# Batch 0's dispatch softmax with tokens in the partitions, in a two-layer attention and slot-expert kernel

## The chip, the cores and the metric

One core of a Trainium2 chip runs the whole program. The metric is the device time of one execution, in microseconds.

## What is computed

The input is `x` of 2 batches by 2048 tokens by 256 features, fp32. First layer: `x = x + layernorm(attention(layernorm(x)))`, an attention of 16 heads with 32 learned patterns in which a sparsemax takes the place of the softmax. Second layer: `x = x + layernorm(slots(layernorm(x)))`, in which 16 slots per batch look at all tokens, go each through an expert of its own, and all tokens look at the 16 slots:

```python
q = jnp.broadcast_to(slot_query, (Bx, NS, D))
o = q + _mha(q, x, x, d_Wq, ...)              # dispatch: 16 slots over 2048 tokens, 16 heads
h = _layernorm(o.reshape(Bx, E, S, D), ...)   # one slot an expert
y = einsum('besf,efd->besd', silu(h @ e_W1 + e_b1) * silu(h @ e_Wg + e_bg), e_W2) + e_b2
o = o + y
out = _mha(x, o, o, c_Wq, ...)                # combine: 2048 tokens over 16 slots
```

The change concerns the dispatch of batch 0. 16 heads times 16 slots make 256 rows ("columns" after the change) of scores over 2048 tokens, each with a softmax over the tokens.

## The kernel before

The four thousand tokens are cut into 32 tiles of 128, in 8 groups of 4 (groups 0 to 3 are batch 0, 4 to 7 batch 1). Every engine has its own program, written out by hand in the order in which it runs; engines wait for each other by counted semaphores (`wait_ge`, `then_inc`). There is no scheduler: what stands in a row on an engine runs in that row, and a wait holds all that stands behind it.

Until about 180 us the kernel makes the sparsemax scores. Then TensorE goes through the heads of batch 1 in steps n = 16 to 33 (the loop `for n in range(KT, 2 * KT + 2)` in the TensorE program, at L1390). Step n has `turn_a(n)` (4 transposes, L1147), `mix(n-1)` (L1157) and `project(n-2)` (L1168), each with a copy by ScalarE between them: `take_a` (L837), `take_h` (L843). VectorE takes the result in `keep_output(n-2)` (L1885, L1887, and L1891 once in four), ScalarE normalises a finished group in `norm_o(g)`, VectorE adds it to `x` and takes its statistics in `join(g)` (L1901, L1656, L1659), GpSimd makes the roots (`roots`, L629 to L634) and ScalarE makes the second norm, `second_norm(g)` (L776), the input of the second layer.

Between these steps lies the dispatch. For a group g, TensorE turns the normed tokens (`turn_norm`, L1194), ScalarE copies them (`put_norm`, L869), TensorE makes the scores (`slot_scores`, L1202: slots in the partitions, 512 tokens in a row, two halves m of 128 slots), and ScalarE keeps them in `s_all` (`put_slot_scores`, L875). VectorE takes each half's maximum over the row (`group_maximum`, L1914). With all four groups of batch 0 there, `batch_maximum` makes one maximum a row (L1918, L1920) and ScalarE makes the exponentials of all 2048 tokens with their sum (`exponential`, L879, twice). The probabilities have slots in the partitions, but the product with the tokens sums over tokens, so they are turned: `turn_p(n)` (four transposes, L1217), copied by `put_probabilities(n)` (L897), and used by `mix_p(n)` (L1231), n = 0 to 7 for batch 0, 8 to 15 for batch 1. `to_slots(0, step)` makes the slots of it. Batch 1 goes the same way in two parts, groups 4 and 5 early (`early_maximum`, `exponential_of_part(False, m)`, L885), 6 and 7 late.

SyncE starts all loads of expert weights (`fetch(n)`) into places that come free, in a fixed row, each behind the wait that frees its place. 21 places are filled ahead of the experts, which start at about 302 us; the later loads wait for `up_ps` or `down_ps` of earlier experts. At the end, from about 400 us, the combine runs.

In the rows, `keep_output(30)` is the L1885 at 239.76 us, `project(n)` is a pair of L1168, and PEld is the weight load that belongs to a PE row.

## Time and profile before

| | us |
|---|---|
| median of 3 runs | 463.04 |
| lowest, highest | 462.29, 465.19 |
| the profiled execution, its own time | 461.39 |
| its span in the profile | 459.7 |
| TensorE busy | 397.7 (87%) |
| VectorE busy | 310.2 (67%) |
| ScalarE busy | 225.3 (49%) |
| GpSimd busy | 147.3 (32%) |

The profile is of one execution, which was 1.65 us faster than the median. The span leaves out 1.7 us at the ends. Busy shares are means over stages with different limits, so they do not say what bounds a stage.

### The profile page before, as it was taken

The page shows a single profiled execution, that of the slowest core. Times are in us where ns is not written, and L with a number is a line of the kernel's source. Part 1 is how long each engine was busy: PE and PEld are TensorE (multiplying, and loading weights), DVE is VectorE, ACT ScalarE, POOL GpSimd, SP SyncE. Part 2 cuts the span into 40 slices and gives each one's busy share as a digit, 9 for nine tenths or more (in the row PEclk, how much of TensorE's full clock was granted, in tenths as well). Part 3 has the DMA queues.
Part 4 walks back from the last instruction along what each step waited for, and adds up shares of the span by engine and source line. Part 5 has one row for each costly group of instructions (what it writes and reads, how often), then busy time and mean ns, then how long its engine had stood idle before and what let it go on. Part 6 is the DMA issues. An engine that isn't in the chain of part 4 may idle for free. (4 is left out here: it accounts for less than half of the span.)

```text
span 459.7 us, 6977 instructions
## 1 busy us (share of the span) xinstructions
PE 397.7 (87%) x2086; PEld 245.7 (53%) x2086; DVE 310.2 (67%) x1189; ACT 225.3 (49%) x413; POOL 147.3 (32%) x243
## 2 busy tenths in 40 slices
PE   7987757589799988999999898999998679999983
PEld 4543223235455454665867666634443237888872
DVE  4899899989999986675425324333334125979996
ACT  2445746748778787878575633100000010355761
POOL 4134465482957522333212100010000000345353
PEclk9997787979989998999999899999999899999999
DMA  7931011011010228448539936979999999701215
GB/s 246 289 124 46 1 46 46 1 46 48 1 46 3 75 97 280 147 151 285 185 135 324 364 139 218 365 249 400 385 404 377 397 378 344 282 0 47 85 54 183
DMA packets 45055, 83.78 MB, mean 182 GB/s; under 512 B 2007, under 2 KB 36445, under 8 KB 40797
## 3 DMA queue, kind: packets, MB, share of 16 engines
q1 hardware_dynamic: 44722, 83.16, 51.7%
q8 instruction: 17, 0.28, 0.2%
q10 hardware_dynamic: 298, 0.21, 0.2%
q14 instruction: 18, 0.14, 0.1%
HBM read 70.78 MB, written 12.58 MB: 181 GB/s over the span
## 5 line engine op out<-in xcount | busy, mean ns | idle before, releaser
L1135 PE MATMUL bank<-Wz,yT 128*128 128x512 f32 x128 | 70.3, 701 | 19.1 <-DVE top L1739 18.9
L1135 PEld LDWEIGHTS bank<-Wz,yT 128*128 128x128 f32 x128 | 27.9, 226 | 54.7 <-issue 44.9
L1739 DVE MAX8 top<-bank 128x8 f32<-128x32 f32 x512 | 51.6, 178 | 1.3 <-ACT arena L798 1.1
L1071 ACT ACTIVATE d<-d 128x32 f32<-128x32 f32 x16 | 3.7, 229 | 84.7 <-DVE d L2127 84.7
L1168 PE MATMUL bank<-aWo,hoT 128*128 128x256 f32 x128 | 37.0, 412 | 0.2 <-DVE arena L1885 0.2
L738 POOL TENSOR_TENSOR work<-work 128x512 f32<-128x512 f32 x16 | 16.6, 1059 | 63.1 <-DVE work L2202 63.1
L1231 PE MATMUL bank<-d,work 128*128 128x256 f32 x128 | 31.9, 397 | 1.6 <-ACT d L897 1.6
L629 POOL TENSOR_SCALAR veps<-mv 128x4 f32<-128x4 f32 x24 | 5.9, 244 | 78.6 <-DVE mv L1659 53.7
L1591 PE MATMUL bank<-scr,work 128*128 128x256 f32 x128 | 29.1, 381 | 1.6 <-ACT work L1084 1.6
L1202 PE MATMUL bank<-arena,Wd 128*128 128x512 f32 x64 | 29.2, 599 | 1.5 <-ACT arena L869 1.5
L1567 PE MATMUL bank<-scr,arena 128*128 128x256 f32 x128 | 28.9, 380 | 0.0
L776 ACT ACTIVATE arena<-arena,shift,rstd 128x256 f32<-128x256 f32 x52 | 26.9, 595 | 3.5 <-POOL shift L634 3.5
L1231 PEld LDWEIGHTS bank<-d,work 128*128 128x128 f32 x128 | 25.2, 205 | 4.9 <-ACT d L897 2.1
L1168 PEld LDWEIGHTS bank<-aWo,hoT 128*128 128x128 f32 x128 | 22.2, 193 | 9.8 <-issue 6.2
L1591 PEld LDWEIGHTS bank<-scr,work 128*128 128x128 f32 x128 | 24.2, 190 | 5.3 <-ACT work L1084 2.1
L2116 DVE TENSOR_TENSOR d<-bank,slotT 128x4 f32 (+1 forms) x16 | 2.6, 165 | 35.2 <-PE bank L1497 35.2
L1157 PE MATMUL bank<-heads 128*64 128x256 f32 x128 | 21.8, 420 | 4.6 <-ACT heads L837 2.6
L632 POOL TENSOR_TENSOR rstd<-veps,mhalf 128x4 f32<-128x4 f32 x24 | 24.9, 1037 | 2.0
L1567 PEld LDWEIGHTS bank<-scr,arena 128*128 128x128 f32 x128 | 23.6, 190 | 3.5 <-DVE scr L2160 0.3
L1885 DVE TENSOR_TENSOR arena<-bank,Wz 128x256 f32<-128x256 f32 x16 | 6.7, 421 | 25.3 <-PE bank L1168 25.2
L1479 PE MATMUL bank<-arena,top 128*32 128x512 f32 x96 | 21.0, 598 | 2.2 <-DMA above<-in_L_ffn_e_Wg_dram 2.2
L659 POOL TENSOR_TENSOR d<-arena,past 128x1024 f32<-128x1024 f32 x8 | 15.1, 1912 | 24.0 <-DVE past L1753 24.0
(295 smaller groups left out, 880.6 us busy)
## 6 DMA issues: line engine op xcount, KB each, us to landing
arena<-in_L_ffn_e_W_dram SPq DMA_DIRECT2D x10, 1024.0 KB, 8.4
x<-in_L_ffn_e_W_dram SPq DMA_DIRECT2D x7, 1024.0 KB, 6.3
scr<-in_L_ffn_e_W_dram SPq DMA_DIRECT2D x7, 1024.0 KB, 13.7
arena<-in_L_ffn_e_Wg_dram SPq DMA_DIRECT2D x6, 1024.0 KB, 9.7
work<-in_L_ffn_e_W_dram SPq DMA_DIRECT2D x5, 1024.0 KB, 12.5
x<-in_L_attn_query_dram SPq DMA_DIRECT2D x1, 4096.0 KB, 16.5
out_dram<-x SPq DMA_DIRECT2D x8, 512.0 KB, 4.4
...
```

Source lines behind the costliest of these rows:

```text
L632: pool.tensor_tensor(rstd[:, k, :], veps[:, k, :], mhalf[:, :], ALU.pow).then_inc(root[k], 1)
L738: pool.tensor_tensor(pv, pv, crs[:, u * 32:(u + 1) * 32].unsqueeze(2).broadcast_to([P, 32, NE]), ALU.mult)\
L776: return act.activation(dst, src, ACT.Identity, bias=shift[:, k, t:t + 1], scale=rstd[:, k, t:t + 1])
L1135: mm = pe.matmul(bZ[t % 2][:, :], yT[:, c, t * P:(t + 1) * P], Wz[:, c, :], start=(c == 0), stop=(c == C - 1))
L1157: mm = pe.matmul(psH[64 * a:64 * a + 64, :], bdh[:, n % TG, :], quarter[:, :, a, :], start=True, stop=True)
L1168: mm = pe.matmul(psO, hoT[:, n % 2, m, :], aWo[:, m, :], start=(m == 0 and n >= KT), stop=(m == 1))
L1202: mm = pe.matmul(bT[m][:, :], Wd[:, c, m * P:(m + 1) * P], ynT[:, g, c, :], start=(c == 0), stop=(c == C - 1))
L1231: mm = pe.matmul((bZ[0] if n < 8 else bank[7])[:, c * 2 * P:(c + 1) * 2 * P], yn[:, kt, c::C], pT[:, n % 2, u * 2 * P:(u + 1) * 2 * P], st ...
L1479: mm = pe.matmul(bank[q][32 * k:32 * k + 32, :], hcol[:, q, c, :], pair[g][c][half], start=(c == 0), stop=(c == C - 1))
L1567: mm = pe.matmul(ps, ynT[:, j, c, t * P:(t + 1) * P], Wc[:, b, c, :], start=(c == 0), stop=(c == C - 1))
L1591: mm = pe.matmul(ps, cpT[:, u, (v * 2 + m) * P:(v * 2 + m + 1) * P], Vc[:, b, m, :], start=(m == 0), stop=(m == 1))
L1739: mx = v.max(top[:, h * TG + t, :], bZ[t % 2][:, h * NS:(h + 1) * NS])
```

## The change

For groups 0 to 3, `slot_scores` puts tokens in the partitions and the 256 slot columns in a row (two tiles of 128 tokens to a bank). No probability of batch 0 is turned: `mix_p(0)` to `(7)` read `s_all` itself. In exchange maximum and sum go over partitions:

- `column_maximum(g)`: VectorE reduces a group's 4 tiles to 256 column maxima for each partition, with a step of 1 KB between the elements that are compared. `three_maxima` joins groups 0 to 2.
- `turn_largest` (TensorE) turns these maxima and those of group 3; `batch_maximum` (VectorE) reduces them to one a slot and puts them on a diagonal; `spread_largest` (TensorE) multiplies that by a square of ones, which GpSimd sets, so that every partition has all 256 maxima.
- `lessen(g)` (VectorE) subtracts them, `exponential(g)` (ScalarE) takes one group at a time, without a sum.
- `sum_up(g)` and `sum_groups` (VectorE) sum in the same strided way, `sum_all` (TensorE) sums over the partitions.

`join(5)` moves from step 28 to step 29. Line numbers in the rows of the order are each kernel's own.

```diff
+
+        largest = d[:, 1024:2048].rearrange("p (g n) -> p g n", g=GB)
+        sums = largest
+        largest3 = above[:, :].bitcast(F32)[:, 0:D]
+        on_diagonal = y[:, 0, :].rearrange("p (m n) -> p m n", m=2)
+        ones_square = y[:, 1, 0:P]
+        total0 = y[:, 2, :]
+        def of_group(g):
+            return s_all[:, :, g * GT:(g + 1) * GT]
+
+        def by_tile(g):
+            return of_group(g).rearrange("p u (v n) -> p u v n", v=2)
+
+        def by_column(g):
+            return of_group(g).rearrange("p u (v n) -> p n u v", v=2)
...
-        NMX = 2 * GB + 2
+        NMX = GB + 4
...
-            sp.wait_ge(pT_ps, KT)
+            sp.wait_ge(pT_ps, KT // 2)
...
+            pool.wait_ge(settled, NB)
+            pool.memset(ones_square, 1.0).then_inc(squared, 1)
...
             def put_slot_scores(g):
                 at = (g % GB) * GT
+                if g >= GB:
+                    act.wait_ge(summed, g - GB + 1)
                 for m in range(2):
                     act.wait_ge(s_ps, g * 2 + (m + 1))
                     act.activation(s_all[:, m, at:at + GT], bT[m][:, :], ACT.Copy).then_inc(s_sb, 1)
 
-            def exponential(m):
-                act.wait_ge(maxed, NMX)
-                act.activation(s_all[:, m, :], s_all[:, m, :], ACT.Exp, bias=nmax[:, m:m + 1],
-                               accum_out=ssum[:, m:m + 1]).then_inc(exped, 1)
+            def exponential(g):
+                act.wait_ge(lessened, g + 1)
+                act.activation(of_group(g), of_group(g), ACT.Exp).then_inc(exped0, 1)
...
             def put_probabilities(n):
-                act.wait_ge(pT_ps, n + 1)
-                if n >= 2:
+                act.wait_ge(pT_ps, n - KT // 2 + 1)
+                if n == KT // 2:
+                    act.wait_ge(summed, GB + 1)
+                if n >= KT // 2 + 2:
 
                     act.wait_ge(g_ps, n - 1)
-                act.activation(pT[:, n % 2, :], (bZ[1] if n < KT // 2 else bA[n % 2])[:, :], ACT.Copy).then_inc(pT_sb, 1)
+                act.activation(pT[:, n % 2, :], bA[n % 2][:, :], ACT.Copy).then_inc(pT_sb, 1)
...
-                if n in (25, 26):
-                    exponential(n - 25)
-                if 27 <= n < 34:
-                    put_probabilities(n - 27)
+                if n in (27, 28, 30, 32):
+                    exponential((27, 28, 30, 32).index(n))
                 if n in (23, 27, 30):
                     norm_o(n // TG - 1)
...
                 if n in (31, 33):
                     put_slot_scores(4 if n == 31 else 5)
-            put_probabilities(7)
             for m in range(2):
                 exponential_of_part(False, m)
...
             def slot_scores(g):
 
                 pe.wait_ge(ynT_sb, 2 * (g + 1))
+                if g < GB:
+
+                    for t in range(TG):
+                        for c in range(C):
+                            mm = pe.matmul(bT[t // 2][:, t % 2 * D:(t % 2 + 1) * D], ynT[:, g, c, t * P:(t + 1) * P], Wd[:, c, :],
+                                           start=(c == 0), stop=(c == C - 1))
+                        if t % 2:
+                            mm.then_inc(s_ps, 1)
+                    return
                 for m in range(2):
                     for c in range(C):
                         mm = pe.matmul(bT[m][:, :], Wd[:, c, m * P:(m + 1) * P], ynT[:, g, c, :],
                                        start=(c == 0), stop=(c == C - 1))
                     mm.then_inc(s_ps, 1)
 
+            def turn_largest():
+
+                pe.wait_ge(maxed, GB + 1)
+                for m in range(2):
+                    for part_, rows_ in enumerate((largest3, largest[:, GB - 1, :])):
+                        mm = pe.transpose(bZ[1][:, (m * 2 + part_) * P:(m * 2 + part_ + 1) * P], rows_[:, m * P:(m + 1) * P],
+                                          ident[:, :])
+                mm.then_inc(largest_ps, 1)
+
+            def spread_largest():
+                pe.wait_ge(squared, 1)
+                pe.wait_ge(maxed, NMX)
+                pe.matmul(bZ[1][:, 0:D], ones_square, on_diagonal, start=True, stop=True).then_inc(largest_ps, 1)
+
+            def sum_all():
+                pe.wait_ge(summed, GB + 1)
+                for m in range(2):
+                    mm = pe.matmul(bZ[1][:, m:m + 1], total0[:, m * P:(m + 1) * P], unit[:, :], start=True, stop=True)
+                mm.then_inc(largest_ps, 1)
+
             def turn_p(n):
                 b, k = n // (KT // 2), n % (KT // 2)
-                if n in (0, 8, 12):
-                    pe.wait_ge(exped, {0: 2, 8: 4, 12: 6}[n])
-                if 1 <= n < 8:
-                    pe.wait_ge(pT_sb, n)
+                if n in (8, 12):
+                    pe.wait_ge(exped, {8: 2, 12: 4}[n])
                 if n >= 10:
-                    pe.wait_ge(pT_sb, n - 1)
-                ps = bZ[1] if n < 8 else bA[n % 2]
+                    pe.wait_ge(pT_sb, n - 9)
                 for u in range(2):
                     for m in range(2):
-                        mm = pe.transpose(ps[:, (u * 2 + m) * P:(u * 2 + m + 1) * P],
+                        mm = pe.transpose(bA[n % 2][:, (u * 2 + m) * P:(u * 2 + m + 1) * P],
                                           s_all[:, m, (2 * k + u) * P:(2 * k + u + 1) * P], ident[:, :])
                 mm.then_inc(pT_ps, 1)
 
             def mix_p(n):
-                pe.wait_ge(pT_sb, n + 1)
+                if n < 8:
+                    pe.wait_ge(exped0, n // 2 + 1)
+                    rows_ = s_all[:, n % 2, GT * (n // 2):GT * (n // 2 + 1)]
+                else:
+                    pe.wait_ge(pT_sb, n - 7)
+                    rows_ = pT[:, n % 2, :]
...
                         mm = pe.matmul((bZ[0] if n < 8 else bank[7])[:, c * 2 * P:(c + 1) * 2 * P], yn[:, kt, c::C],
-                                       pT[:, n % 2, u * 2 * P:(u + 1) * 2 * P],
+                                       rows_[:, u * 2 * P:(u + 1) * 2 * P],
                                        start=(kt == first and c == 0), stop=(kt == end - 1 and c == C - 1))
                 mm.then_inc(g_ps, 1)
...
-                if 27 <= n < 35:
-                    turn_p(n - 27)
+                if n == 25:
+                    turn_largest()
+                if n == 26:
+                    spread_largest()
                 if 28 <= n < 35:
                     mix_p(n - 28)
                 if n in (30, 32):
                     turn_norm(4 if n == 30 else 5)
                 if n in (31, 33):
                     slot_scores(4 if n == 31 else 5)
-            turn_p(7)
             mix_p(6)
             mix_p(7)
             turn_p(8)
             turn_p(9)
+            sum_all()
             mix_p(8)
...
+            def column_maximum(g):
+
+                v.wait_ge(s_sb, 2 * g + 2)
+                v.tensor_reduce(largest[:, g, :], by_column(g), AX_XY, ALU.max).then_inc(maxed, 1)
+
+            def three_maxima():
+                v.wait_ge(maxed, GB - 1)
+                v.tensor_reduce(largest3, largest[:, 0:GB - 1, :].rearrange("p g n -> p n g"), AX_X, ALU.max).then_inc(maxed, 1)
+
             def batch_maximum():
-                v.wait_ge(maxed, NMX - 2)
-                v.tensor_reduce(smax[:, :], pmax[:, :, 0:GB], AX_X, ALU.max).then_inc(maxed, 1)
-                v.wait_ge(maxed, NMX - 1)
-                v.tensor_scalar(nmax[:, :], smax[:, :], -1.0, None, ALU.mult).then_inc(maxed, 1)
+                v.wait_ge(largest_ps, 1)
+                v.tensor_reduce(smax[:, :], bZ[1][:, :].rearrange("p (m n) -> p m n", m=2), AX_X, ALU.max).then_inc(maxed, 1)
+                v.wait_ge(maxed, GB + 2)
+                for m in range(2):
+                    v.tensor_scalar(on_diagonal[:, m, :], ident[:, :], smax[:, m:m + 1], None, ALU.mult).then_inc(maxed, 1)
+
+            def lessen(g):
+
+                v.wait_ge(largest_ps, 2)
+                v.tensor_tensor(by_tile(g), by_tile(g), bZ[1][:, 0:D].unsqueeze(1).unsqueeze(1).broadcast_to([P, 2, 2, D]),
+                                ALU.subtract).then_inc(lessened, 1)
+
+            def sum_up(g):
+                v.wait_ge(exped0, g + 1)
+                v.tensor_reduce(sums[:, g, :], by_column(g), AX_XY, ALU.add).then_inc(summed, 1)
+
+            def sum_groups():
+                v.wait_ge(summed, GB)
+                v.tensor_reduce(total0, sums[:, :, :].rearrange("p g n -> p n g"), AX_X, ALU.add).then_inc(summed, 1)
...
                     if b == 0:
-                        v.wait_ge(exped, 2)
-                        v.reciprocal(rsum[:, :], ssum[:, :]).then_inc(slots, 1)
+                        v.wait_ge(largest_ps, 3)
+                        v.reciprocal(rsum[:, :], bZ[1][:, 0:2]).then_inc(slots, 1)
...
             for n in range(KT + 2, 2 * KT + 2):
                 if n == 25:
-                    group_maximum(3)
+                    column_maximum(3)
+                if n == 26:
                     batch_maximum()
+                if n == 27:
+                    lessen(0)
                 keep_output(n - 2)
+                if n in (18, 19, 23):
+                    column_maximum((18, 19, 23).index(n))
+                if n == 23:
+                    three_maxima()
+                if n in (28, 30, 31):
+                    lessen((28, 30, 31).index(n) + 1)
+                if n in (30, 32, 33):
+                    sum_up((30, 32, 33).index(n))
                 if n == 20:
                     join_add(3)
                 if n == 21:
                     join_statistics(3)
                 if n == 22:
-                    group_maximum(0)
-                    group_maximum(1)
-                if n == 23:
-                    group_maximum(2)
-                if n == 22:
                     v.wait_ge(w_in2, 16 * N_W2)
                     own(v.tensor_tensor(sq[:, :], sq[:, :], dbo, ALU.add))
-                if n in (24, 28):
+                if n in (24, 29):
                     join(4 if n == 24 else 5)
                 if n == 32:
...
             group_maximum(5)
             early_maximum()
+            sum_up(3)
+            sum_groups()
             to_slots(0, 0)
             join(7)
```

What else the diff has: names for the new views and semaphores, and the smaller counts of `exped`, `maxed` and `pT_sb` behind these edits.

VectorE, from the group maximum of group 3 to the third step after it. `pmax<-work` is the group maximum, `arena<-bank,Wz` a `keep_output`. Before:

```order
L1659 BN_AGGR mv<-stats 128x2 x4
L1914 TENSOR_REDUCE pmax<-work 128x1 x2
L1918 TENSOR_REDUCE smax<-pmax 128x2
L1920 TENSOR_SCALAR nmax<-smax 128x2
L1885 TENSOR_TENSOR arena<-bank,Wz 128x256
L1887 BN_STATS stats<-arena 128x6
L1891 BN_AGGR mv<-stats 128x2 x4
L1885 TENSOR_TENSOR arena<-bank,Wz 128x256
```

The same place now; `d<-work` is the column maximum, `smax<-bank` and `y<-ident,smax` are `batch_maximum`, `work<-work,bank` is `lessen(0)`:

```order
L1716 BN_AGGR mv<-stats 128x2 x4
L1976 TENSOR_REDUCE d<-work 128x256
L1942 TENSOR_TENSOR arena<-bank,Wz 128x256
L1944 BN_STATS stats<-arena 128x6
L1948 BN_AGGR mv<-stats 128x2 x4
L1984 TENSOR_REDUCE smax<-bank 128x2
L1987 TENSOR_SCALAR y<-ident,smax 128x128 x2
L1942 TENSOR_TENSOR arena<-bank,Wz 128x256
L1944 BN_STATS stats<-arena 128x6
L1992 TENSOR_TENSOR work<-work,bank 128x2x512
```

The maximum of the batch now stands behind a `keep_output`, since it waits for TensorE's transposes.

VectorE, from `keep_output(30)` on. Before:

```order
L1885 TENSOR_TENSOR arena<-bank,Wz 128x256
L1887 BN_STATS stats<-arena 128x6
L1914 TENSOR_REDUCE pmax<-work 128x1 x2
L1901 TENSOR_TENSOR x<-x,arena 128x1024
L1656 BN_STATS stats<-x 128x6 x4
L1659 BN_AGGR mv<-stats 128x2 x4
L1885 TENSOR_TENSOR arena<-bank,Wz 128x256
```

The same place now, where `d<-work` is `sum_up(1)` and then `sum_up(2)`:

```order
L1942 TENSOR_TENSOR arena<-bank,Wz 128x256
L1944 BN_STATS stats<-arena 128x6
L1997 TENSOR_REDUCE d<-work 128x256
L1971 TENSOR_REDUCE pmax<-work 128x1 x2
L1958 TENSOR_TENSOR x<-x,arena 128x1024
L1713 BN_STATS stats<-x 128x6 x4
L1716 BN_AGGR mv<-stats 128x2 x4
L1942 TENSOR_TENSOR arena<-bank,Wz 128x256
L1944 BN_STATS stats<-arena 128x6
L1948 BN_AGGR mv<-stats 128x2 x4
L1997 TENSOR_REDUCE d<-work 128x256
```

A sum of 1024 elements stands ahead of `join(6)`, and a second one behind `keep_output(31)`.

## Rows read from the trace of the kernel before

**Rows 1.** Stretch, us, busy PE, PEld, DVE, ACT, POOL; PEclk, DMA share, GB/s

```profile
228.00:240.00 12.00, 11.48 (x57) 7.47 (x55) 1.09 (x3) 7.68 (x16) 2.85 (x8) 1.00 0.28 92
...
250.00:256.00 6.00, 4.30 (x23) 3.42 (x22) 2.35 (x8) 5.22 (x11) 0.00 (x0) 1.00 0.92 288
256.00:270.00 14.00, 13.05 (x55) 9.80 (x56) 4.17 (x11) 6.89 (x14) 1.89 (x5) 0.88 0.79 281
...
350.00:380.00 30.00, 21.17 (x188) 9.55 (x188) 7.35 (x24) 2.43 (x6) 0.19 (x1) 0.94 1.05 384
```

**Rows 2.** VectorE's groups by shape: busy us, mean ns of one

```profile
L2189 DVE TENSOR_TENSOR work<-bank,work 128x512 f32<-128x512 f32 x16 | 11.1, 691 | 0.6
...
L1914 DVE TENSOR_REDUCE pmax<-work 128x1 f32<-128x512 f32 x16 | 10.2, 676 | 17.0 <-ACT work L875 17.0
L1901 DVE TENSOR_TENSOR x<-x,arena 128x1024 f32<-128x1024 f32 x8 | 9.7, 1216 | 2.7 <-ACT arena L776 2.7
...
L1801 DVE TENSOR_REDUCE tot<-past 128x1 f32<-128x64 f32 x5 | 1.1, 211 | 0.0
...
L1705 DVE TENSOR_REDUCE sel<-ident 128x32 f32<-128x128 f32 x1 | 0.4, 372 | 0.0
L1706 DVE TENSOR_REDUCE sel<-ident 128x16 f32<-128x128 f32 x1 | 0.4, 366 | 0.0
```

**Rows 3.** Timeline of steps 28 and 29: start, us, instruction [idle before]

```profile
216.85 1.13 PE L1168 MATMUL bank<-aWo,hoT 128*128 128x256 f32 x4
...
217.82 0.60 PE L1217 MATMUL bank<-ident,work 128*128 128x128 f32 x4
...
218.26 1.90 PE L1231 MATMUL bank<-d,work 128*128 128x256 f32 x8
...
221.10 1.13 PE L1168 MATMUL bank<-aWo,hoT 128*128 128x256 f32 x4
```

**Rows 4.** Timeline of steps 23 to 27

```profile
200.17 1.13 PE L1168 MATMUL bank<-aWo,hoT 128*128 128x256 f32 x4
...
203.43 1.10 PE L1168 MATMUL bank<-aWo,hoT 128*128 128x256 f32 x4 [0.17 <-DVE arena L1885]
...
208.92 1.13 PE L1168 MATMUL bank<-aWo,hoT 128*128 128x256 f32 x4
...
211.00 1.13 PE L1168 MATMUL bank<-aWo,hoT 128*128 128x256 f32 x4
...
215.25 0.66 PE L1217 MATMUL bank<-ident,work 128*128 128x128 f32 x4 [0.18 <-ACT work L879]
```

**Rows 5.** Timeline, the first chain

```profile
224.51 2.07 ACT L776 ACTIVATE work<-x,shift,rstd 128x256 f32<-128x256 f32 x4 [1.20 <-PE bank L1231]
...
226.80 0.23 POOL L629 TENSOR_SCALAR veps<-mv 128x4 f32<-128x4 f32 x1 [12.68 <-ACT work L776]
...
231.29 2.08 ACT L776 ACTIVATE arena<-arena,shift,rstd 128x256 f32<-128x256 f32 x4 [3.48 <-POOL shift L634]
...
234.38 3.70 PE L1202 MATMUL bank<-arena,Wd 128*128 128x512 f32 x8 [0.52 <-ACT arena L869]
```

**Rows 6.** Timeline, the second chain

```profile
239.76 0.42 DVE L1885 TENSOR_TENSOR arena<-bank,Wz 128x256 f32<-128x256 f32 x1 [7.15 <-PE bank L1168]
...
241.74 1.22 DVE L1901 TENSOR_TENSOR x<-x,arena 128x1024 f32<-128x1024 f32 x1
...
244.50 0.38 DVE L1659 BATCH_NORM_AGGREGATE mv<-stats 128x2 f32<-128x6 f32 x4
...
247.01 2.07 ACT L776 ACTIVATE work<-x,shift,rstd 128x256 f32<-128x256 f32 x4 [2.23 <-POOL shift L634]
...
248.99 1.05 ACT L875 ACTIVATE work<-bank 128x512 f32<-128x512 f32 x2
...
253.59 2.06 ACT L776 ACTIVATE arena<-arena,shift,rstd 128x256 f32<-128x256 f32 x4
...
256.18 3.65 PE L1231 MATMUL bank<-d,work 128*128 128x256 f32 x8 [1.35 <-ACT d L897]
```

12 lines of the change are left out of this document (9 added, 3 removed).

## The prediction

> **What bounds the kernel now.** I read the stretch table first (busy time and granted clock by stretch), then the instructions in order of time from 193 to 304 us, then the groups by shape for prices. The stretches show a kernel of two halves [rows 1]. From 304 us on the 16 experts run: the DMA engines are full (share 1.05 in 350 to 380 us), and later loads are released by earlier experts, so this half begins when the slots are ready and ends a fixed time later. What the change touches lies before it, and a shift of its end shifts everything behind it one for one, because transfers are not full there and each waits for a step of this half. In 228 to 240 us TensorE is busy 11.48 of 12 us: it is almost, but not wholly, the bound. What ends last has to be read step by step.
>
> A step n of the second batch's heads has `turn_a(n)`, `mix(n-1)`, `project(n-2)`. Without other work a step takes 2.08 us (L1168 starts at 208.92 and 211.00, [rows 4]). With a `turn_p` and a `mix_p` it takes 4.25 us (216.85 to 221.10, [rows 3]), so `turn_p` is 0.43 us (217.82 to 218.26) and `mix_p` 1.7 us.
>
> Two chains run beside TensorE. The first: `mix_p(1)` lets ACT start `second_norm(4)` at 224.51, GpSimd waits 12.68 us for it, and its two groups of roots let ACT start `norm_o(6)` at 231.29; after `put_norm(4)`, `slot_scores(4)` starts at 234.38, TensorE having waited 0.52 us [rows 5]. The second: VectorE, idle 7.15 us, takes `keep_output(30)` at 239.76, then the maximum of group 4, then `join(6)` (241.74 to 244.88). GpSimd's roots follow, ACT waits for them and starts `second_norm(6)` at 247.01, and only behind it `put_slot_scores(5)` at 248.99. From there it goes by the maximum and two exponentials to `norm_o(7)` and `put_probabilities(8)`, for which TensorE waits until 256.18 [rows 6].
>
> **The change, part by part.**
>
> *Matmuls of scores.* 4 products of 512 columns a group become 8 of 256. By columns that is the same work, 2048 before and after: 0. ACT's two copies stay.
>
> *Transposes.* 8 `turn_p` go, 3.4 us of TensorE; `turn_largest` (4 transposes, 0.43) and `spread_largest` (one product of 256 columns, a quarter of `mix_p`, 0.43) come. `turn_p(7)` lay in the shadow of the second chain and saves nothing, nor do `turn_p(2)` to `(6)` where a chain ends last. What counts is when `project(27)` comes, because the first chain hangs on it.
>
> *ACT.* Two exponentials of 2048 elements, for the last of which `turn_p(0)` waited and started only at 215.25 [rows 4], become four of 1024, spread out. The 8 copies go. ACT is not late anywhere in this stretch after that: gain included below.
>
> *VectorE.* Instead of 8 maxima of 512 elements (676 ns each, [rows 2]) there are 4 column maxima and 4 column sums of 1024 elements, `three_maxima` of 768, `sum_groups` of 1024, one reduce of 512 from PSUM, two scalings of 128 and 4 `lessen` of 1024. `lessen` is known: 0.14 + 1024 x 1.04 = 1.2 us as in L1901 and, with broadcast and PSUM, twice the slope of L2189. The column reduces are not: they step 1 KB from element to element. Two contiguous reduces give 0.144 us + 1.038 ns an element (64 elements 211 ns, 512 elements 676 ns). At that price a column reduce costs C = 1.21 us. The only reduces that step between elements are those of `ident`, 128 elements in 366 and 372 ns, where the line gives 277 [rows 2]. Put on the slope, this is 1.78 ns an element and C = 1.97 us; put down to a fixed cost it would be C = 1.30. Both strides there, 64 and 128 bytes, cost the same, so I take it that what costs is leaving the neighbourhood and not how far: C = 1.97, `three_maxima` 1.51.
>
> The Trainium skill has two rules here that disagree. "VectorE: DVE Perf Modes", Mode 1x, says that the baseline mode takes fp32 with any strides at one result a cycle; by it the sum would be that of C = 1.21. "SBUF — State Buffer", in its note on cachelines (Door 1), says that every access which goes to a new 16-byte line pays a penalty; that speaks against this change. The two rows on `ident` agree with the second page, as far as 128 elements can.
>
> *The sum.* (1) VectorE is free to take `keep_output(21)` at 201.30 (200.17 + 1.13), since the maxima of groups 0 and 1 moved to idle time at steps 18 and 19; the wait of 0.17 us at `project(22)` goes [rows 4], so `project(23)` starts at 208.75. (2) VectorE then has, in order, `keep_output(21)` 0.8, the column maximum of group 2, `three_maxima`, `keep_output(22)` 0.8, `join(4)` 3.1 and the column maximum of group 3: 201.35 + 0.8 + 1.97 + 1.51 + 0.8 + 3.1 + 1.97 = 211.5. (3) `turn_largest` stands behind `project(23)` and could start at 209.7: TensorE waits 1.8 to 2.0 us, and everything behind it on its queue (step 26 on) with it. (4) From `project(23)` to `project(27)` there are now 4 steps of 2.08, 0.43, 0.43 and one `mix_p` of 1.7: 10.9 us. So `project(27)` starts at 208.75 + 10.9 + 1.9 = 221.6 instead of 221.10: **+0.5**. The 3.4 us of transposes and the waits for the exponentials pay for the new wait and no more. (5) The first chain: `join(5)` has moved from step 28 to 29 and is done 4.5 us after the end of `project(27)` (`keep_output` with its aggregates 1.3, join 3.1). GpSimd's start at 226.80 was 4.6 us after it. So the chain keeps its length, `slot_scores(4)` comes at +0.5, and the further `turn_p` only make TensorE wait longer before it. (6) The second chain: `sum_up(1)` stands between `keep_output(30)` and the maximum of group 4, with `join(6)`, the roots, `second_norm(6)` and `put_slot_scores(5)` behind it. Nothing hides it, since VectorE sat idle until `keep_output(30)` could start: **+1.97**. (7) `sum_up(3)`, `sum_groups` (3.9 us) and `sum_all` stand ahead of the copies of `to_slots(0,0)` and of `join(7)`, and `put_probabilities(8)` now waits for `sum_groups`. They run during the two exponentials and `norm_o(7)`, about 4.4 us, which hold that copy anyway; that leaves 0.4 us. Behind `join(7)`, `second_norm(7)` has about a microsecond of slack: 0. If that cover were gone, each microsecond of the sums would come on top. (8) SP's fetches 18 and 19 wait for the same transpose as before (the count is halved with the transposes), and GpSimd's memset is once 128 elements: 0.
>
> Sum: +0.5 + 1.97 = **+2.5 us**. On the profiled execution, 461.4 us (span 459.7), that is 463.9; the median of the runs shown, 463.0, lies 1.6 above it, so I forecast 465.5.
>
> **The rivals.**
>
> *A: column reduces at the contiguous price.* Then VectorE is done at 201.35 + 0.8 + 1.21 + 0.94 + 0.8 + 3.1 + 1.21 = 209.4, TensorE does not wait, `project(27)` comes 1.5 us early, and `sum_up(1)` takes 1.21 back: -0.3, so 462.7. With a fixed cost only (C = 1.30): +0.0. For it: nothing in the profile shows a slow contiguous reduce. Against it: the `ident` rows. The Mode 1x rule of the Trainium skill ("VectorE: DVE Perf Modes") would lead here.
>
> *B: slower by over 1%.* The stride costs two cycles and more, say 2.08 ns an element, twice the contiguous slope; C = 2.28 and `three_maxima` 1.74. VectorE is done at 212.4, TensorE waits 2.7 us at `turn_largest`, `project(27)` is at +1.2, `sum_up(1)` adds 2.28: +3.5. A wait of that length may cost more: in 250 to 256 us TensorE was busy 4.30 of 6, and in the 14 us after it the granted clock was 0.88 [rows 1], that is 3.4 us at its lower level (1.2 GHz), 1.7 us of work lost. With one such fall on the path, +5.2: 468.2. It decides from C = 2.1 with a fall, or from 2.5 without one, since the end grows by 3.75 us for each of C (2.75 ahead of `turn_largest`, 1 in `sum_up(1)`). A fall beside C = 1.97 gives +4.2: 467.2. The Trainium skill ("TensorE: Matmul & The Clock Gate", HAM oscillation) has waits between matmuls throttle the clock; the drop to 0.88 agrees.
>
> *C: faster by over 1%.* All 8 transposes would have to be on the path (3.4 us) with the fall at 256 us gone too (1.7): -5.1, so 457.9. The two chains speak against it.
>
> *D: the change does not do what it says.* The order of each engine has the new instructions where the code puts them and the removed ones nowhere; it gets no chance of its own.
>
> **How the numbers follow.** Forecast 0.55, its own range 464.3 to 467.0 (C from 1.7 to 2.2, half a microsecond of the shown runs' scatter). A 0.25, B 0.16, C 0.04. The range 462.0 to 468.8 takes in A and most of B. A measurement of this kernel tells about 1% (4.6 us) from no change. Faster: C, 0.04. Slower: most of B and a tail of the forecast with a fall, 0.16. The rest, 0.80, is within 1%: C of either price gives less than that.
>
> **What would show it.** Right: column reduces of 1.9 to 2.0 us; TensorE waiting about 2 us for VectorE before the four transposes of the maxima, and over 2 us for ACT before `slot_scores(4)`; VectorE without a gap from `keep_output(30)` to `join(6)`, ending 2.5 us later than 244.88; the copy at the start of the experts 2.5 us later than now. Wrong: column reduces of 1.2 us; `second_norm(6)` not waiting for GpSimd; the granted clock below 1 between 212 and 250 us; or an expert half whose length changes.

## The result, and the profile after

| | before | changed |
|---|---|---|
| median (15 runs each) | 462.18 us | 465.43 us |
| lowest to highest | 460.25 to 465.19 | 463.48 to 468.24 |
| profiled execution, its span | 461.39, 459.7 | 464.68, 463.0 |

The ratio is 1.0074, 95% interval 1.0058 to 1.0089: slower by 0.74%, so within 1%. Ratios here and below leave out executions more than 1.5% above the fastest of their kernel; medians keep all. With a dozen executions or more a kernel's times spread over 4 to 7 us, so a profile is one draw, and I compare lengths of stages between profiles and medians between runs.

The groups of VectorE's new operations in the changed kernel, all between 185 and 262 us (line, engine, operation, operands, count | busy us, mean ns | idle before):

```profile
L1997 DVE TENSOR_REDUCE d<-work 128x256 f32<-128x1024 f32 x4 | 7.9, 1978 | 0.0
L1976 DVE TENSOR_REDUCE d<-work 128x256 f32<-128x1024 f32 x4 | 7.9, 1973 | 0.0
...
L1992 DVE TENSOR_TENSOR work<-work,bank 128x1024 f32<-128x1024 f32 x4 | 4.8, 1204 | 0.0
...
L2001 DVE TENSOR_REDUCE y<-d 128x256 f32<-128x1024 f32 x1 | 1.9, 1941 | 0.0
...
L1980 DVE TENSOR_REDUCE above<-d 128x256 f32<-128x768 f32 x1 | 1.0, 1036 | 0.0
```

The column maxima (L1976) and sums (L1997) cost 1.97 and 1.98 us, the price taken from the two `ident` rows in [rows 2]. `lessen` (L1992) costs 1.2 us as L1901 did there. But `three_maxima` (L1980) costs 1.04 us, not 1.51.

TensorE in the changed kernel around the new steps, against [rows 4] and [rows 5] (start, duration, then what; in brackets the idle time before and who ended it):

```profile
190.03 1.10 PE L1192 MATMUL bank<-aWo,hoT 128*128 128x256 f32 x4 [0.28 <-DVE arena L1942]
...
200.64 1.13 PE L1192 MATMUL bank<-aWo,hoT 128*128 128x256 f32 x4
...
203.70 1.13 PE L1192 MATMUL bank<-aWo,hoT 128*128 128x256 f32 x4
...
209.23 1.13 PE L1192 MATMUL bank<-aWo,hoT 128*128 128x256 f32 x4
211.47 0.33 PE L1244 MATMUL bank<-ident,above 128*128 128x128 f32 x1 [1.11 <-DVE d L1976]
...
234.71 3.70 PE L1235 MATMUL bank<-arena,Wd 128*128 128x512 f32 x8 [1.82 <-ACT arena L893]
...
255.98 1.97 PE L1267 MATMUL bank<-ident,work 128*128 128x128 f32 x8 [3.78 <-ACT work L910]
...
258.45 3.76 PE L1286 MATMUL bank<-d,work 128*128 128x256 f32 x8
```

`project(21)` (the L1192 at 200.64) is already 0.47 us behind its 200.17 of [rows 4], before the first step of the prediction's sum. Part of that is the change itself: the 0.28 us at 190.03 are TensorE in front of `project(20)`, waiting for a `keep_output` that stands behind the first column maximum. The small wait in front of `project(22)` is gone. A new one stands at `turn_largest` (L1244). At `slot_scores(4)` (L1235) the wait grew from 0.52 to 1.82 us, but its start moved by 0.33 only: the removed transposes became waiting. At `turn_p(8)` (L1267) the wait is 3.78 us. Before, `turn_p(8)` had 0.52 us, and `mix_p(8)` 1.35 us more [rows 6]:

```profile
253.73 1.09 PE L1217 MATMUL bank<-ident,work 128*128 128x128 f32 x8 [0.52 <-ACT work L885]
```

VectorE's second chain in the changed kernel, in order of time:

```profile
240.09 0.42 DVE L1942 TENSOR_TENSOR arena<-bank,Wz 128x256 f32<-128x256 f32 x1 [6.88 <-PE bank L1192]
...
240.89 2.00 DVE L1997 TENSOR_REDUCE d<-work 128x256 f32<-128x1024 f32 x1
242.79 1.28 DVE L1971 TENSOR_REDUCE pmax<-work 128x1 f32<-128x512 f32 x2
243.98 1.23 DVE L1958 TENSOR_TENSOR x<-x,arena 128x1024 f32<-128x1024 f32 x1
```

`keep_output(30)` comes 0.33 us later than in [rows 6] and `join(6)` (L1958) 2.24 us later. The 1.91 between them is `sum_up(1)`. The delay is passed on unshortened: ACT's `second_norm(6)` starts 2.25 us later, `mix_p(8)` 2.27.

Stretches of the changed kernel, against [rows 1] (stretch, length, busy us of PE, PEld, DVE, ACT and POOL, granted clock, DMA share, GB/s):

```profile
250.00:256.00 6.00, 2.22 (x12) 1.67 (x10) 4.23 (x7) 4.74 (x10) 1.16 (x2) 0.95 0.97 322
256.00:262.00 6.00, 6.00 (x20) 5.18 (x21) 4.67 (x9) 2.85 (x6) 0.00 (x0) 0.50 0.59 228
262.00:270.00 8.00, 7.22 (x32) 4.82 (x31) 1.73 (x7) 4.77 (x9) 1.88 (x5) 0.98 0.81 268
355.00:385.00 30.00, 22.74 (x177) 10.20 (x179) 7.16 (x23) 2.20 (x5) 0.19 (x1) 0.83 1.06 384
```

And of the kernel before, the two whose clock differs most:

```profile
256.00:262.00 6.00, 5.83 (x25) 5.01 (x26) 2.80 (x9) 1.79 (x5) 1.89 (x5) 0.72 1.02 382
...
355.00:385.00 30.00, 21.30 (x179) 11.27 (x180) 8.05 (x31) 2.20 (x5) 0.00 (x0) 0.94 1.04 379
```

After the wait at 252 us TensorE is busy without a gap but at its lower level (1.2 GHz) in all of 256 to 262 us. In the last experts the clock is lower too, 0.83 against 0.94. The experts' first matmul stands at 304.42 (301.97 before, +2.45), the copy of VectorE behind the experts at 388.20 (384.91, +3.29), and from there to the end of the span both kernels take 74.8 us.

### The profile page after: what moved, and what is told of

It is laid out like the page before. It is cut to its first block and busy times, and to the rows that moved or that the text cites. A ratio compares the mean times of both kernels' runs of the same rounds, so it can differ in the third digit from the quotient of the medians.

```text
span 463.0 us, 6991 instructions
## 1 busy us (share of the span) xinstructions
PE 397.0 (86%) x2092; PEld 251.4 (54%) x2096; DVE 328.7 (71%) x1196; ACT 221.5 (48%) x405; POOL 147.6 (32%) x244
## 2 busy tenths in 40 slices
DMA packets 45054, 83.78 MB, mean 181 GB/s; under 512 B 2006, under 2 KB 36444, under 8 KB 40796
## 5 line engine op out<-in xcount | busy, mean ns | idle before, releaser
L1159 PE MATMUL bank<-Wz,yT 128*128 128x512 f32 x128 | 68.3, 684 | 18.2 <-DVE top L1796 18.0
L1192 PE MATMUL bank<-aWo,hoT 128*128 128x256 f32 x128 | 37.5, 417 | 0.3 <-DVE arena L1942 0.3
L1192 PEld LDWEIGHTS bank<-aWo,hoT 128*128 128x128 f32 x128 | 22.3, 194 | 10.0 <-issue 6.3
L1536 PE MATMUL bank<-arena,top 128*32 128x512 f32 x96 | 22.4, 630 | 2.2 <-DMA above<-in_L_ffn_e_Wg_dram 2.2
L861 ACT ACTIVATE heads<-bank 128x512 f32<-128x512 f32 x32 | 18.9, 595 | 11.2 <-PE bank L1171 11.2
L673 POOL TENSOR_TENSOR arena<-arena,past 128x2048 f32 (+1 forms) x4 | 14.5, 3637 | 20.7 <-DVE past L1853 20.7
L1116 ACT ACTIVATE arena<-bank 128x512 f32<-128x512 f32 x16 | 9.5, 596 | 22.5 <-PE bank L1648 22.5
L800 ACT ACTIVATE work<-x,shift,rstd 128x256 f32<-128x256 f32 x32 | 16.6, 590 | 7.5 <-POOL shift L656 5.7
```

The lines of the kernel that those rows point to most:

```text
L800: return act.activation(dst, src, ACT.Identity, bias=shift[:, k, t:t + 1], scale=rstd[:, k, t:t + 1])
L861: act.activation(aT[:, n % 2, :], bA[n % 2][:, :], ACT.Relu).then_inc(a_sb, 1)
L1159: mm = pe.matmul(bZ[t % 2][:, :], yT[:, c, t * P:(t + 1) * P], Wz[:, c, :], start=(c == 0), stop=(c == C - 1))
L1192: mm = pe.matmul(psO, hoT[:, n % 2, m, :], aWo[:, m, :], start=(m == 0 and n >= KT), stop=(m == 1))
L1536: mm = pe.matmul(bank[q][32 * k:32 * k + 32, :], hcol[:, q, c, :], pair[g][c][half], start=(c == 0), stop=(c == C - 1))
```

## The experiments

Theory at the start: VectorE's column reductions at nearly 2 us each, above all the one ahead of `join(6)`, make the loss, and the removed transposes lay beside a wait. Rivals: the place in the row and not the price decides; the granted clock after the longer wait is the real cost. The first eight kernels ran on one chip in two sessions (e1, e2, e3, e7, then e5, e6, e9, e10), the last four on another; each ratio is to the kernel before in the same session.

**The sum in another place (e1).** `sum_up(1)` ahead of `keep_output(30)`, where VectorE sits idle.

```diff
+                if n == 32:
+                    sum_up(1)
...
-                if n in (30, 32, 33):
+                if n in (30, 33):
```

> The changed kernel with sum_up(1) put ahead of keep_output(30), into VectorE's 6.9 us of idle time, nothing else. Theory (the place of that one reduce costs 1.9 us, the rest of the change is about even): put_slot_scores(5), which starts at 251.2 us in the changed kernel, starts about 2.0 us earlier, and the time falls by 1.9 to 2.0 us, to about 463.4 by the median, within 0.3% of the kernel before plus 1.3. Rival (VectorE has simply more to do, 18 us more, and that costs wherever it stands): the time stays within 0.5 us of the changed kernel, 465.4.

Ratio 1.0032 (0.9997 to 1.0067), median 463.88 of 12. `join(6)` starts at 242.05 instead of 243.98, and the experts at 302.31 instead of 304.42. TensorE's waits at `turn_p(8)` and `mix_p(8)` in that profile:

```profile
254.05 1.09 PE L1267 MATMUL bank<-ident,work 128*128 128x128 f32 x8 [1.86 <-ACT work L910]
...
256.49 3.59 PE L1286 MATMUL bank<-d,work 128*128 128x256 f32 x8 [0.39 <-ACT d L924]
```

A step of 2 us that moves by one place gives back 2.1 us. In the profiles this is the one part of the loss that a single edit removes in full. The times show it less surely: six of the twelve lie between 460.1 and 462.3 us and six between 465.5 and 467.5, and the ratio's interval overlaps that of the unchanged form (e12 below, 1.0036 to 1.0093).

**The price alone (e2).** All ten column reductions read four (or three) neighbours in place of columns, so this kernel takes maxima and sums of other elements than it should. The cut shows the view that the eight reductions of a group read; the two others are changed alike.

```diff
-            return of_group(g).rearrange("p u (v n) -> p n u v", v=2)
+            return of_group(g).rearrange("p u (n k) -> p u n k", k=4)
...
```

> The changed kernel with all ten strided reduces made contiguous (each takes four, or three, neighbours; the same counts of elements in and out). The maxima and sums are then those of other elements, so the output is not the reference's. Theory (stride alone costs 0.76 us a reduce of 1024): the reduces take 1.2 us each instead of 1.97, TensorE waits under 0.3 us before turn_largest instead of 1.5, and the time falls by 0.77 in sum_up(1) plus 1.1 to 1.5 at turn_largest, that is 1.9 to 2.3 us, to about 463.3. Rival (the reduce is slow by its 256 results of four elements, not by the stride): the reduces stay at 1.9 us or more and the time does not move.

Ratio 1.0066 (1.0036 to 1.0096), median 463.90 of 12. The groups of the reductions:

```profile
L1976 DVE TENSOR_REDUCE d<-work 128x256 f32<-128x1024 f32 x4 | 4.8, 1206 | 0.0
L1997 DVE TENSOR_REDUCE d<-work 128x256 f32<-128x1024 f32 x4 | 4.8, 1204 | 0.0
...
L2001 DVE TENSOR_REDUCE y<-d 128x256 f32<-128x1024 f32 x1 | 1.2, 1220 | 0.0
L1980 DVE TENSOR_REDUCE above<-d 128x256 f32<-128x768 f32 x1 | 1.0, 953 | 0.0
```

Same instructions, same count of elements, 1.21 instead of 1.97 us: the order of the addresses costs 0.77 us. The group reductions also run over one axis instead of two, but `sum_groups` (L2001) has one axis in both kernels and falls alike, from 1.94 to 1.22. The wait at `turn_largest` is gone; those at `slot_scores(4)` (1.82 us) and `turn_p(8)` (2.99 us) remain. `join(6)` starts at 241.93 and the experts at 302.26, 0.29 us later than before, yet the median stays 2.25 us above the kernel before. That part is not explained by this profile.

**Another form of the same reduction (e3).** Two element-wise operations for each column reduction: halves of 512 elements, then 256.

```diff
...
-                v.tensor_reduce(sums[:, g, :], by_column(g), AX_XY, ALU.add).then_inc(summed, 1)
+                v.tensor_tensor(halves, of_group(g)[:, 0, :], of_group(g)[:, 1, :], ALU.add).then_inc(squared, 1)
+                v.wait_ge(squared, GB + g + 2)
+                v.tensor_tensor(sums[:, g, :], halves[:, 0:D], halves[:, D:2 * D], ALU.add).then_inc(summed, 1)
...
```

> The changed kernel with each column reduce made by two contiguous tensor_tensor (512, then 256 elements), and sum_groups the same way; three_maxima stays. All instructions stay in their places. Theory: 0.69 + 0.42 + a wait, 1.13 to 1.2 us, instead of 1.97; TensorE's wait at turn_largest goes and project(27) comes 1.1 to 1.5 us earlier; sum_up(1) costs 0.8 less; the time falls by 1.9 to 2.3 us, to about 463.3, no faster than the kernel before by more than 0.5. Rival (price of the reduces is hidden, the second chain is set by something else): less than 0.5 us.

Ratio 1.0080 (1.0057 to 1.0103), median 465.44 of 6: nothing gained. The two operations of a sum take 0.68 and 0.46 us, and `join(6)` starts 1.72 us earlier, but the experts only 0.57. What was lost on the way:

```profile
254.43 1.09 PE L1269 MATMUL bank<-ident,work 128*128 128x128 f32 x8 [3.10 <-ACT work L912]
...
256.88 3.78 PE L1288 MATMUL bank<-d,work 128*128 128x256 f32 x8 [1.01 <-ACT d L926]
```

```profile
256.00:262.00 6.00, 5.12 (x16) 4.30 (x17) 3.75 (x12) 1.30 (x3) 1.68 (x5) 0.50 0.88 309
262.00:270.00 8.00, 7.22 (x30) 4.83 (x29) 1.37 (x2) 4.71 (x9) 0.20 (x2) 0.95 0.61 193
```

`turn_p(8)` ran at the upper level, then the clock fell and `mix_p(8)` and its followers ran at 1.2 GHz until 262 us and beyond. The expectation missed because it took the clock's loss as a constant: from `turn_p(8)` to the experts this profile takes 0.98 us longer than that of the changed kernel.

**The prices measured by themselves (e7).** Ten reductions of the same buffer in a row, results unused, in one execution of 477.76 us: 2, 3 and 4 elements a result at a step of 1 KB (L2008), 4 at 1020 and 1008 bytes, 8 at 512, 16 at 256, 256 at 16 bytes, 512 at 8 bytes, and 4 neighbours.

```diff
...
+                for k in (2, 3, 4):
+                    own(v.tensor_reduce(to, src[:, 0:256 * k].rearrange("p (g n) -> p n g", g=k), AX_X, ALU.add))
...
+                own(v.tensor_reduce(to[:, 0:4], src[:, :].rearrange("p (g n) -> p n g", g=256), AX_X, ALU.add))
+                own(v.tensor_reduce(to[:, 0:2], src[:, :].rearrange("p (g n) -> p n g", g=512), AX_X, ALU.add))
+                own(v.tensor_reduce(to, src[:, :].rearrange("p (n g) -> p n g", g=4), AX_X, ALU.add))
...
```

> The changed kernel with ten reduces more on VectorE ahead of keep_output(30), for their durations alone (the results go to unused space): stride 1 KB with 2, 3 and 4 elements a result; 4 elements at 1020 and at 1008 bytes; 8 elements at 512 bytes; 16 at 256; 256 at 16 bytes; 512 at 8 bytes; 4 contiguous. Theory A (the cost is leaving a neighbourhood): everything from 16 bytes up takes 1.75 to 1.8 ns an element. Theory B (since three_maxima at 1 KB took only 1.17 ns an element: the cost comes with strides that make the even count of 4 meet the same place, a bank): 3 elements 1.2 ns, 2 and 4 at 1 KB 1.75 ns, 1020 bytes near 1.04 ns. The time is some 10 us longer, which says nothing.

First the three of L2008 as one line's instructions (shortest, middle, longest in ns), then the others in order of time:

```profile
L2008 DVE TENSOR_REDUCE y<-work x3: 700/1045/1962, 238.9 to 240.7; 128x256 f32<-128x512 f32 x1, 128x256 f32<-128x768 f32 x1, 128x256 f32<-128x1024 f32 x1
```

```profile
242.72 1.90 DVE L2009 TENSOR_REDUCE y<-work 128x255 f32<-128x1020 f32 x1
244.65 1.87 DVE L2010 TENSOR_REDUCE y<-work 128x252 f32<-128x1008 f32 x1
246.55 1.87 DVE L2011 TENSOR_REDUCE y<-work 128x128 f32<-128x1024 f32 x1
248.46 1.87 DVE L2012 TENSOR_REDUCE y<-work 128x64 f32<-128x1024 f32 x1
250.36 1.95 DVE L2013 TENSOR_REDUCE y<-work 128x4 f32<-128x1024 f32 x1
252.34 1.22 DVE L2014 TENSOR_REDUCE y<-work 128x2 f32<-128x1024 f32 x1
253.59 1.22 DVE L2015 TENSOR_REDUCE y<-work 128x256 f32<-128x1024 f32 x1
```

The steps tried from 16 bytes to 1 KB make hardly a difference: 1.87 to 1.96 us for about 1024 elements. At 8 bytes it is 1.22, as for neighbours. (The number of elements in a result changes along with the step, so the two are not separated.) With only 2 or 3 elements a result at 1 KB it is 0.70 and 1.05 us, near the contiguous price: the slope gives 0.144 + 512 x 1.038 ns = 0.68 for the first, and e2's contiguous reduction of 768 took 0.95. Theory A held from four elements on and failed at two and three; theory B failed at 1020 bytes.

**The clock held in the wait (e5), and the same in the kernel before (e6).** Matmuls of the kernel's own warming kind (`keep_clock`, results unused), twelve in e5 and ten in e6, between `mix_p(7)` and `turn_p(8)`. The wait for `o_sb` holds them until VectorE has taken the last `project`.

```diff
             mix_p(7)
+            pe.wait_ge(o_sb, 2 * KT)
+            keep_clock(7, 12)
             turn_p(8)
```

> The changed kernel with twelve matmuls of the warming kind (each 0.2 us, results unused) between mix_p(7) and turn_p(8), where TensorE waits 3.78 us for ScalarE and its granted clock then stands at the lower level from 255.3 to 262.2 us. Theory A (the wait costs more than its length, through the clock): turn_p(8) starts at 256.0 as now, takes 1.09 instead of 1.97 us, the clock in 256 to 262 is 1.00, turn_norm(6) starts 1.0 to 2.0 us earlier than 262.01, and the experts' first matmul stands at 302.4 to 303.5 instead of 304.42. Theory B (the way through that stretch is set by VectorE and ScalarE, the clock costs nothing there): the clock is 1.00 and the experts still start at 304.2 to 304.6. Theory C (the clock falls anyway at the next short wait): turn_p(8) takes 1.09, mix_p(8) is slow, nothing won.

> The kernel before with ten such matmuls at the same place, where it waits only 0.52 and then 1.35 us and its clock is at the lower level from about 256 to 259.3 us. If the clock in that stretch is a cost that both kernels carry, this one gains nearly what the changed kernel gains: mix_p(8) takes 2.1 instead of 3.65 us, experts' first matmul at 300.8 to 301.3 instead of 301.97. If only the changed kernel's longer wait costs clock, it gains under 0.4 us here or loses up to 0.5 us, since ten matmuls last 2.1 us and the gap is 0.52.

e5: ratio 1.0058 (1.0022 to 1.0093), median 464.44 of 7. e6: 0.9987 (0.9960 to 1.0014), 461.13 of 12. In e5's profile:

```profile
255.93 1.09 PE L1267 MATMUL bank<-ident,work 128*128 128x128 f32 x8 [1.20 <-ACT work L910]
...
258.38 2.00 PE L1286 MATMUL bank<-d,work 128*128 128x256 f32 x8 [0.39 <-ACT d L924]
```

```profile
256.00:262.00 6.00, 5.25 (x34) 4.76 (x35) 5.13 (x13) 3.44 (x8) 0.00 (x0) 1.00 0.67 239
```

`turn_p(8)` starts where it did (255.93), takes 1.09 instead of 1.97 us, `mix_p(8)` 2.00 instead of 3.76, and the experts start at 302.51: -1.91, theory A. In e6 they start at 300.62, -1.35 to the kernel before. So the clock there is a cost that both kernels carry, not one that the change brought. Neither gain shows in the medians beyond their intervals.

**The clock held in the last experts (e9, e10).** Eight such matmuls ahead of the first step (`grow`) of experts 13 to 15, in the changed kernel and in the one before.

```diff
+                if e in (13, 14, 15):
+                    keep_clock(q, 8)
                 pair = [weights(e, 0), weights(e, 1)]
```

> The changed kernel with eight warming matmuls ahead of the grow step of experts 13, 14 and 15, where TensorE waits 2 to 3.5 us for weights and where, in the profiles so far, the clock was at its lower level once or twice between 355 and 382 us, in another expert each time. Theory: the clock's level there decides 1.0 of the 3.3 us by which the profiled span of the changed kernel is longer. Then the clock in 355 to 382 is 1.00 throughout, the offset to the kernel before stays 2.2 to 2.5 us from 305 us to the end, the median falls by about 1 us and the spread of the times shrinks. Rival: DMA sets the pace there (its share is over 1.0) and the clock fall is hidden: clock 1.00, median unchanged within 0.4 us.

> The kernel before with the same eight matmuls at the same three places. If the lower clock in the last experts is a matter of the moment that both kernels have in some executions, this one too gains about 0.5 to 1 us in the median and its spread shrinks, and e9 minus e10 is 2.2 to 2.5 us. If only the changed kernel loses there, this one does not change, and e9 minus the kernel before is 2.2 to 2.5 us.

e9: ratio 1.0089 (1.0062 to 1.0116), median 464.94 of 6. e10: 0.9978 (0.9953 to 1.0002), 460.53 of 12. The clock is 1.00 in both, here in e9:

```profile
355.00:385.00 30.00, 24.98 (x212) 12.43 (x212) 7.17 (x24) 2.20 (x5) 0.19 (x1) 1.00 1.06 385
```

Between the experts' first matmul and the copy behind them e9 takes 82.48 us, e10 82.59. With the clock equal, the two kernels' expert halves have the same length in these two profiles; the spans are 461.9 and 459.4. The change in the medians was not seen as expected: e9's ratio is no lower than that of the changed kernel itself. e10's did fall by 0.8 us, within its interval.

**Both remedies (e4), with the clock held (e8), and the kernel before with the clock held in both places (e11).** e4 is e3 and e1 together. e8 adds six warming matmuls before `turn_p(8)`, those of e9, and `join(5)` back at step 28. e11 is e6 and e10 together. e12 is the changed kernel again.

```diff
...
-                if n in (24, 29):
+                if n in (24, 28):
                     join(4 if n == 24 else 5)
```

> Both remedies together on the changed kernel: every column reduction of VectorE as two element-wise operations, and the sums over group 1's tokens taken ahead of keep_output(30). Theory (the added 2.3 us ahead of turn_p(8) are VectorE's column reductions in front of join(6), at 1.97 us each): join(6) starts near 240.5 us instead of 243.98 (1.7 less by the trees as in e3, 2.0 less by the order as in e1, less what they share), turn_p(8) near 252.7, its wait falls to about 1.5 us, and with that short wait the experts start at 301.0 to 302.0, so not later than in the kernel before (301.97) by more than 0.1; the time is 462 to 463 us, ratio 0.999 to 1.004. Rival (a wait on ScalarE or DMA takes over once VectorE is early): join(6) as said, experts not before 302.2, ratio over 1.004.

> The same with join(5) back at step 28, six warming matmuls in the wait ahead of turn_p(8), and eight at each of experts 13 to 15. Theory: clock 1.00 from 250 to 270 and from 355 to 382 us, experts' first matmul at 300.3 to 301.3, offset to the kernel before at the end of the experts (its copy at 384.91) -0.5 to -1.5 us, time 461 to 462 us, and no better than the kernel before with the same warming matmuls, since the new scores took nothing off the path that this one still pays. Rival: the removed copies of ScalarE and transposes show once VectorE and the clock are out of the way; then it is over 0.5 us ahead of e11_before_both at the same place.

> The kernel before with both sets of warming matmuls. By the profiles of e6 and e10: experts' first matmul at 300.6, offset at the end of the experts -1.5 to -1.8 us (in e6 the gain of 1.35 fell to 0.28 while the clock was at its lower level from 363 to 375), time 459.5 to 460.5 us, ratio 0.995 to 0.998. If DMA sets the pace of the experts whatever the clock does, the offset at their end is -0.2 to -0.5 as in e6 and e10 alone.

> The changed kernel as it is, on the same chip as the three others, to have medians that can be set beside each other: 464.5 to 466 us, ratio 1.006 to 1.009, experts' first matmul 304.2 to 304.7, turn_p(8) behind a wait of 3.6 to 3.9 us and at the lower clock. The offset at the end of the experts is open: 2.3 us if the clock holds in the last three, up to 3.7 us if it falls in one of them.

| | ratio (95%) | median, runs |
|---|---|---|
| e4 | 1.0021 (0.9992 to 1.0050) | 462.28, 12 |
| e8 | 0.9970 (0.9941 to 0.9998) | 461.37, 12 |
| e11 | 0.9977 (0.9936 to 1.0017) | 460.92, 9 |
| e12 | 1.0064 (1.0036 to 1.0093) | 465.34, 12 |

e12 repeats the loss. Nine of its twelve times lie between 464.5 and 467.4 us and three between 461.0 and 462.2, and its profiled execution (462.23, span 460.4) is one of the three. The changed kernel's own profile (464.68) is 2.6 us longer in span: 1.04 up to `slot_scores(3)`, 0.50 from `turn_p(8)` to the experts and 1.01 in the expert half. What makes others last 466 us and more is in no profile of that kernel. e4's median is as expected; its profiled execution (466.43) was one of its slowest, and its experts start at 306.02, not at the expected 301 to 302. It shows the clock falling at another wait that had cost nothing in the others:

```profile
236.09 5.40 PE L1237 MATMUL bank<-arena,Wd 128*128 128x512 f32 x8 [2.05 <-ACT arena L895]
...
257.35 1.97 PE L1269 MATMUL bank<-ident,work 128*128 128x128 f32 x8 [2.06 <-ACT work L912]
```

`slot_scores(4)` lasts 5.40 instead of 3.70 us behind a wait of 2.05; in e3's profile the same wait was 2.04 and the matmuls took 3.70. e8 missed in its clock: six matmuls were too few, the clock in 256 to 262 us was 0.72, and it was 2.2 us late at `slot_scores(3)` already. Still it has the lowest ratio of the versions with the new scores, 0.3% ahead of the kernel before with an interval that ends just short of none, and level with e11, whose profile was 2.7 us late there too. So the repaired new kernel and the old one can't be told apart once both have warming matmuls; by the table below e11 is 0.73 us shorter from `slot_scores(3)` to the experts.

Lengths of stages in all profiles but e7's, each from the starts of its rows (us); the stages are `slot_scores(3)` to `turn_p(8)`, from there to the experts' first matmul, and on to the copy behind the experts, with the granted clock of 256 to 262 and 355 to 385 us:

| | to `turn_p(8)` | to experts | to the copy | clock | clock |
|---|---|---|---|---|---|
| before | 49.36 | 48.24 | 82.94 | 0.72 | 0.94 |
| e10 | 49.39 | 48.25 | 82.59 | 0.72 | 1.00 |
| e6 | 50.83 | 45.42 | 84.00 | 1.00 | 0.77 |
| e11 | 50.87 | 45.42 | 83.23 | 1.00 | 1.00 |
| changed | 51.31 | 48.44 | 83.78 | 0.50 | 0.83 |
| e12 | 51.31 | 47.94 | 82.77 | 0.65 | 0.83 |
| e9 | 51.32 | 48.43 | 82.48 | 0.50 | 1.00 |
| e5 | 51.29 | 46.58 | 83.51 | 1.00 | 0.89 |
| e1 | 49.40 | 48.26 | 83.37 | 0.72 | 0.83 |
| e2 | 49.49 | 48.34 | 83.24 | 0.67 | 0.83 |
| e3 | 50.25 | 49.42 | 84.26 | 0.50 | 0.89 |
| e4 | 50.93 | 48.67 | 83.91 | 0.61 | 0.83 |
| e8 | 48.78 | 48.24 | 82.85 | 0.72 | 1.00 |

The first column is where the change costs: 1.95 us, the same in e12, e9 and e5 (in e5 the warming matmuls fit into the wait), and gone in e1. (In e6 and e11 it holds the ten warming matmuls as well.) The second differs by 0.20 between the two kernels, and falls by 1.9 to 2.8 only where the clock was held. The third moves by 1.5 us (82.77 to 84.26) among the nine profiles with the same expert code, and by 1.01 between the changed kernel and e12, which are one kernel with the same clock of 0.83. What differs there is where the lower level lies: in 5 us stretches the clock was 0.81, 0.50 and 0.67 in 365 to 380 us of the first, and 0.92, 0.50 and 0.56 in 355 to 370 us of the second. Whether the place decides was not tested.

## Why the prediction was right

The forecast was +2.5 us on the profile (463.9) and 465.5; it came to 464.68 and 465.43. The mechanism held, and part of the agreement in size is luck. 465.5 was 463.0 plus 2.5; the kernel before came out at 462.18 over 15 executions, and the medians differ by 3.25. So the base was taken 0.8 us too high and the change 0.75 too low, and the two errors cancel.

- Step (1) held in its main point: the wait of 0.17 us is gone, and `project(21)`'s 0.47 us of delay shrinks to 0.27 and 0.31 at `project(22)` and `(23)`. But the maxima of groups 0 and 1 did not lie wholly in idle time: the first made TensorE wait 0.28 us at `project(20)`.
- Step (2) ends at 211.42 where 211.5 was said, by two errors that cancel: VectorE began 0.5 us later, since `project(21)` was late, and `three_maxima` took 1.04 instead of 1.51.
- Step (3): the wait at `turn_largest` was 1.11 and not 1.8 to 2.0 us. Part of this is a way of counting: the bracket counts from the modelled end of `project(23)`, the forecast from 0.97 us after its start, and by that count the wait was 1.27. The rest is TensorE's later arrival, since `project(23)` started at 209.23 and not at 208.75. With TensorE on time VectorE would have ended 0.5 us sooner too, since `three_maxima` was 0.47 us cheaper than priced, so the cheap `three_maxima` is what made the wait shorter than forecast.
- Step (4) was mis-sized by the same term: `project(27)` starts at 221.47, +0.37, and less the 0.47 that is -0.1 where +0.5 was forecast. The transposes paid for the new wait and a little more.
- Step (5) held in kind: the chain kept its length and TensorE waited 1.82 us ahead of `slot_scores(4)` (over 2 were named as a sign), whose start moved by 0.33.
- Step (6), the main term, held: +1.91 for +1.97, and e1 shows it by undoing it.
- Step (7): the later sums were hidden; from `mix_p(8)` (+2.27) to the experts' start (+2.45) 0.18 us were added.
- Not in the sum: 0.47 us at 200 us and 0.84 in the expert half. Of the first, 0.35 stood at `project(18)`, ahead of VectorE's first new instruction; TensorE had been 0.93 behind at 147 us, ahead of every new one. I had said that an expert half whose length changes would make me wrong. It changed, but e12, the changed kernel again, has it 0.17 us shorter than the kernel before, and e9 and e10 have it equal to 0.11 us. It belongs to one execution and not to the change. That the clock is what moves it is likely and not shown.

So the change's own part in the profile is 2.45 - 0.47 = 2.0 us counted from `project(21)`, or 2.15 from `slot_scores(3)`, where I said 2.5, and the rest of the 3.29, all but the part of the early delay at `project(20)`, came by itself. The medians differ by 3.25 and, on e12's chip, 3.76 us. The interval of the first (2.7 to 4.1 us) lies above these 2.0 to 2.15, that of e12 (1.7 to 4.3) contains them. A like excess stands in e1 and e2: their profiles reach the experts 0.3 us after the kernel before, their medians lie 2.2 us above its. So the experiments show the 2 us, and leave the rest of the medians open.

The clock is a possible source, since the changed kernel has longer waits (1.11, 1.82 and 3.78 us for 0.17, 0.52, 0.52 and 1.35), and e4's profile shows lower levels behind its waits of 2 us. The granted clock over whole executions fits: its mean is 0.940 in the changed kernel (15 executions) and 0.948 in the kernel before (23, beside e1), and in e12 as in e4 the four slowest executions have 0.935 to 0.939 and the three fastest 0.945 or more. But the fastest of the 15 has 0.935, and e5 holds the clock at one of the waits and its median (ratio 1.0058) can't be told from e12's. A second source lies ahead of the change: `slot_scores(3)` starts anywhere from 203.63 to 207.06 us in these profiles, and e11 was 3.2 us late at `slot_scores(0)` (149.90 for 146.70), in code that is the same in all. So the rest is argued and not shown.

Rival A's price is what e2 bought: the wait at `turn_largest` is gone there, and the experts start at +0.29 where A's sum gave -0.3. Rival B's price (2.08 ns an element) was wrong. The clock did not fall behind `turn_largest`, where B had it; it stayed at 1.00 from 204 to 250 us. It fell at `turn_p(8)`, as before, and by the stretches' clock the lower level lasted 6.9 us instead of 3.4, but that cost only 0.2 us more on the way to the experts. Rival C had all removed transposes on the path; `slot_scores(4)` at +0.33 speaks against that. "A shift of its end shifts everything behind it one for one" fits a delay (+2.11 us from `slot_scores(3)` to the experts between e10 and e9, -0.11 behind) but not a gain: e11 reaches the experts 1.35 us sooner than e10 by the same count and then takes 0.64 longer. Each is one pair of profiles, and one kernel's two profiles differ by 1.01 us there, so neither is shown.

The Trainium skill ("SBUF — State Buffer", the note on cachelines at Door 1) has accesses that leave a 16-byte line pay. The step from 1.22 us at 8 bytes to 1.95 at 16 agrees (though a result there is made of 512 and of 256 elements). By the same page of the Trainium skill 2 or 3 elements a result at 1 KB would pay as well, and they pay 0.1 us at most (0.70 and 1.05 us). The rule of Mode 1x in the Trainium skill ("VectorE: DVE Perf Modes"), one result a cycle at any stride, fails for this reduction by 0.75 us in 1.96.
